# Values added by tiles on GpSimd, one product with the constant matrix, and the text rows gathered batch by batch

## What is computed

```python
h = concat([scharr_edges(gray(x)), (U * s @ Vt)[x_txt]], axis=1)   # (16, 384, 256)
# attention, 16 heads, window of 128 rows back, on layernorm(h)
attn = softmax(where(mask, scores, -10000.0)) + 1e-9
h = h + (attn @ v) @ Wo.T + bo
# the 288 highest rows of 384 by a router score pass gelu(x @ w_block)
h = h + mixture_of_depths(layernorm(h))
# state space: h_t = ifft(lambda * fft(h_{t-1})).real + B u_t ; y = C h_t + D u_t
h = h + ssm(layernorm(h))
# shared expert + top 2 of 8 experts, 256 -> 1024 -> 256
h = h + shared_ffn(x3) + sum_of_two_experts(x3)
```

## Time and profile before

| | us |
|---|---|
| median of 3 runs | 2071.47 |
| lowest, highest | 2069.86, 2071.95 |
| the profiled execution | 2072.98 |
| its span, first to last instruction | 2071.20 |
| 0 to 229.2: start, sequences 0 and 1 | 229.2 |
| 229.2 to 1213: twelve sequences in the loop | 983.8 |
| 1213 to 1436: the last sequences | 223.0 |
| 1436 to the end: experts | 635.2 |

### The profile page before, as it was taken

The page is one execution under the profiler, slowest core; times in us unless marked ns, Lnnn a source line. Parts: engine busy times, 40 slices in busy tenths (PEclk is TensorE's granted clock), DMA queues, the critical chain, the costliest instruction groups (busy, mean ns, idle before and its releaser), DMA issues.

```text
span 2071.2 us, 45656 instructions
## 1 busy us (share of the span) xinstructions
PE 1918.9 (93%) x14039; PEld 1626.8 (79%) x14120; DVE 1358.2 (66%) x3782; ACT 1066.4 (51%) x2510; POOL 782.1 (38%) x1269
## 2 busy tenths in 40 slices
PE   3679999999999999999999999888999999999997
PEld 3456777777777777777777777667999999999997
DVE  4657676777777777777777767654665565555653
ACT  0346455555555554555655655541664554655643
POOL 4012333343243233332432432324454454545544
PEclk8789999999999999999999999999999999999999
DMA  4320220211202212112122021111532232323222
GB/s 133 82 53 26 62 55 23 69 43 41 69 23 61 59 32 54 52 32 69 32 52 67 24 61 38 24 57 36 164 89 45 41 89 46 85 44 89 46 44 40
DMA packets 81092, 116.58 MB, mean 56 GB/s; under 512 B 20964, under 2 KB 61508, under 8 KB 78724
## 3 DMA queue, kind: packets, MB, share of 16 engines
q1 hardware_dynamic: 54372, 84.16, 15.1%
q0 software_dynamic: 23360, 27.91, 8.0%
q10 hardware_dynamic: 3312, 3.94, 0.6%
HBM read 51.58 MB, written 26.71 MB: 38 GB/s over the span
## 4 chain that ended last, share of the span: by engine, by line
PE 63%; issue 12%; DVE 11%; POOL 9%; ACT 2%; DMA 1%; POOLq 1%; ACTq 1%; DVEq 0%
PE ps L1956 14%; PE ps L1764 7%; PE ps L1968 5%; PE ps L1969 5%; PE ps L1967 5%; PE ps L1635 4%; POOL slot_rows L695 4%; PE ps L1607 3%; PE ps L1692 3%; PE ps L1712 2%; PE ps L1684 2%; PE ps L1754 2%; PE ps L1815 2%; PE ps L1777 2%; PE ps L1749 2%
## 5 line engine op out<-in xcount | busy, mean ns | idle before, releaser
L838 ACT ACTIVATE prob<-ps,mx 128x256 f32<-128x256 f32 (+1 forms) x768 | 294.3, 441 | 204.3 <-DVE mx L1194 198.6
L957 ACT ACTIVATE hid_hi<-ps,b 128x256 fp32r<-128x256 f32 x408 | 203.4, 499 | 286.3 <-PE ps L1956 286.3
L1194 DVE TENSOR_REDUCE mx<-ps 128x2 f32<-128x512 f32 (+1 forms) x384 | 227.6, 597 | 161.9 <-PE ps L1684 140.4
L1537 DVE TENSOR_TENSOR hid_lo<-hid_full,hid_hi 128x256 fp32r<-128x256 f32 x408 | 171.5, 425 | 145.7 <-ACT hid_full L960 142.0
L830 ACT ACTIVATE pT<-ps 128x512 f32<-128x512 f32 (+1 forms) x384 | 202.0, 531 | 120.3 <-PE ps L1692 79.4
L751 POOL DMA_INDIRECT result<-yb,idx_o x102 | 177.2, 1737 | 172.5 <-DVE yb L1554 150.7
L1967 PE MATMUL ps<-w_hi,hid_hi 128*128 128x256 f32 x816 | 233.5, 286 | 0.0
L1969 PE MATMUL ps<-w_hi,hid_lo 128*128 128x256 f32 x816 | 229.4, 281 | 0.0
L1968 PE MATMUL ps<-w_lo,hid_hi 128*128 128x256 f32 x816 | 229.3, 281 | 0.0
L1692 PE MATMUL ps<-ident,prob 128*128 128x128 f32 x1280 | 208.3, 277 | 6.2 <-ACT prob L838 6.0
L1684 PE MATMUL ps<-ks,qs 96*128 96x512 f32 (+1 forms) x384 | 201.3, 524 | 4.2 <-ACT prob L838 4.2
(11 more groups left out here) (310 smaller groups left out, 4244.0 us busy)
## 6 DMA issues: line engine op xcount, KB each, us to landing
w_raw<-in_w SPq DMA_DIRECT2D x16, 1024.0 KB
xin<-in_x SPq DMA_DIRECT2D x32, 384.0 KB
ks<-k_hi SPq DMA_DIRECT2D x256, 48.0 KB, 2.1
qs<-q_hi SPq DMA_DIRECT2D x120, 96.0 KB, 2.2
ks<-k_lo SPq DMA_DIRECT2D x128, 48.0 KB, 2.1
xn_rows<-xc SPq DMA_DIRECT2D x16, 384.0 KB, 2.5
result<-h SPq DMA_DIRECT2D x16, 384.0 KB
qs<-q_lo SPq DMA_DIRECT2D x60, 96.0 KB, 2.2
```

The costliest lines, as they stand in the source:

```text
L838: ins = act.activation(prob[:, s % PB, hh, w], ps[:, s % 2, hh * 2 * P + w.start:(hh + 1) * 2 * P], ACT.Exp, bias=mx[:, s % 2, hh:hh + 1])
L957: act.activation(hid_hi[:, f], ps[:, f % 4, 0:CHUNK], ACT.Gelu_apprx_tanh, bias=b1[half][:, f:f + 1])
L1194: dve.tensor_reduce(mx[:, s % 2], sc, AX_X, ALU.max, negate=True).then_inc(max_done.sem, 1)
```

## The change

The sum over the tiles of v is made by two additions on GpSimd (vsum), and TensorE makes one product in slot SUMV = 6 in place of three; VectorE copies it in slot 7. gather_text(b+2) is issued in GpSimd's sequence b, between dispatch and chain_deviations, through a copy of the batch's column of ids, into one buffer u_rows; batch 1 is gathered at the start. powers uses st for its helper rows, and the wait for the stacks in slot 1 of sequence 0 goes. split_router moves to slot 15 of sequence 0.

```diff
+SUMV = 6
-        u_all = sb("u_all", [P, NB, R])
+        id_col = sb("id_col", [P, 1], I32)
+        u_rows = sb("u_rows", [P, R])
+        vsum = room("vsum", [P, D])
...
         @block.gpsimd
-            def gather_text(b, done):
-                pool.indirect_dma_start(u_all[:, b, :], None, t["U"],
-                                        bass.IndirectOffsetOnAxis(ids[:, b:b + 1], axis=0)
-                                        ).then_inc(done.sem, 16)
+            def gather_text(b):
+                pool.wait_ge(ub_ready.sem, ub_ready.at(b - 1, 1))
+                pool.tensor_copy(id_col[:], ids[:, bass.ds(b, 1)]).then_inc(id_ready.sem, 1)
+                pool.wait_ge(id_ready.sem, id_ready.at(b - 1, 1))
+                pool.sem_inc(pool_go.sem, 1)
+                pool.indirect_dma_start(u_rows[:], None, t["U"], bass.IndirectOffsetOnAxis(id_col[:, 0:1], axis=0)
+                                        ).then_inc(u_gathered.sem, 16)
...
+            def add_values(b):
+
+                heads = vsum[:].rearrange("p (h d) -> p h d", h=NH)
+                pool.wait_ge(v_ready.sem, v_ready.at(b, 1))
+                pool.tensor_tensor(heads, vaug[:, 0, :, 0:DK], vaug[:, 1, :, 0:DK], ALU.add).then_inc(vsum_step.sem, 1)
+                pool.wait_ge(vsum_step.sem, vsum_step.at(b, 1))
+                pool.tensor_tensor(heads, heads, vaug[:, 2, :, 0:DK], ALU.add).then_inc(vsum_ready.sem, 1)
+
+            def sequence(b, att, late, chain, head, ahead):
+                if att:
+                    add_values(b)
                 if late and att:
                     dispatch(b - 2)
+                if ahead:
+                    gather_text(b + 2)
                 if chain:
                     if att:
                         chain_deviations(b - 1, 1)
...
-            for b in range(1, NB):
-                gather_text(b, u_gathered)
+            gather_text(1)
             residual(0)
...
-            sequence(0, True, False, False, True)
+            sequence(0, True, False, False, True, True)
...
+            with pool.Fori(2, NB - 2) as b:
+                sequence(b, True, True, True, True, True)
+            sequence(NB - 2, True, True, True, True, False)
...
         @block.scalar
             def text_rows(b):
                 act.wait_ge(uT_ready.sem, uT_ready.at(b, 0))
-                act.activation(ub[:, 0:R], u_all[:, bass.ds(b, 1), :], ACT.Copy).then_inc(ub_ready.sem, 1)
+                act.wait_ge(u_gathered.sem, u_gathered.at(b, 16))
+                act.activation(ub[:, 0:R], u_rows[:], ACT.Copy).then_inc(ub_ready.sem, 1)
...
-            act.wait_ge(u_gathered.sem, u_gathered.at(0, 16 * (NB - 1)))
             sequence(0, True, False, False, True, first=True)
...
         @block.vector
             def powers(n):
-                dve.tensor_scalar(rot[:, 0, 0:m], turn[:, 0, 0:m], re, None, ALU.mult)
-                dve.tensor_scalar(rot[:, 1, 0:m], turn[:, 0, 0:m], im, None, ALU.mult)
+                dve.tensor_scalar(st[:, 0, 0:m], turn[:, 0, 0:m], re, None, ALU.mult)
+                dve.tensor_scalar(st[:, 1, 0:m], turn[:, 0, 0:m], im, None, ALU.mult)
...
                     if first and s == 1:
                         eigenvalues()
-                        for pair in range(PAIRS):
-                            dve.wait_ge(stacked[pair].sem, stacked[pair].at(b, stacked[pair].per))
...
-                    if att and s == 2:
+                    if att and s == SUMV + 1:
                         values_sum(b)
...
                     if first and s == CONV:
+                        split_router()
                         split_shared()
...
-            dve.wait_ge(late_loaded.sem, late_loaded.at(0, NLATE))
-            split_router()
             sequence(1, True, False, True, True, True)
...
         @block.tensor
-            def values_sum(b, first, last):
-
-                pe.wait_ge(v_ready.sem, v_ready.at(b, 1))
+            def values_sum(b):
+
+                pe.wait_ge(vsum_ready.sem, vsum_ready.at(b, 1))
                 pe.wait_ge(h1_ready.sem, h1_ready.at(b, 0))
-                for i in range(first, last):
-                    ins = pe.matmul(ps[:, 5, D:2 * D].rearrange("p (h d) -> p h d", h=NH), ones9[:], vaug[:, i, :, 0:DK],
-                                    start=(i == 0), stop=(i == NT - 1))
-                if last == NT:
-                    ins.then_inc(sumv_done.sem, 1)
+                pe.matmul(ps[:, 5, D:2 * D], ones9[:], vsum[:], start=True, stop=True).then_inc(sumv_done.sem, 1)
...
-                    if att and s == BLOCK:
-                        values_sum(b, 1, NT)
                     if late and s == BLOCK:
                         down(b - 2, 0, chained, head)
...
-                    if att and s == TURN0:
-                        values_sum(b, 0, 1)
+                    if att and s == SUMV:
+                        values_sum(b)
```

More of the change, by code:

```diff
@@ L292, in build @@
         ids_loaded = dma_signal("ids_loaded", 0)
-        u_first = dma_signal("first_u_gathered", 0)
-        u_gathered = dma_signal("u_gathered", 0)
+        u_gathered = dma_signal("u_gathered", 16)
+        id_ready = signal("text_id_ready", 1)
         ub_zeroed = signal("ub_zeroed", 0)
@@ L318, in build @@
         v_ready = signal("v_ready", 1)
+        vsum_step = signal("tiles_of_values_added", 1)
+        vsum_ready = signal("vsum_ready", 1)
         sumv_done = signal("sumv_done", 1)
@@ L605, in _ @@
         def _(pool):
-            def gather_text(b, done):
-                pool.indirect_dma_start(u_all[:, b, :], None, t["U"],
-                                        bass.IndirectOffsetOnAxis(ids[:, b:b + 1], axis=0)
-                                        ).then_inc(done.sem, 16)
+            def gather_text(b):
[5 more added lines that the diff above has]
+                                        ).then_inc(u_gathered.sem, 16)
             pool.wait_ge(ids_loaded.sem, ids_loaded.at(0, 16))
-            gather_text(0, u_first)
+            pool.indirect_dma_start(u_rows[:], None, t["U"], bass.IndirectOffsetOnAxis(ids[:, 0:1], axis=0)
+                                    ).then_inc(u_gathered.sem, 16)
             pool.wait_ge(band_ready.sem, band_ready.at(0, 1))
@@ L718, in sequence @@
                     residual(b + 1)
-            for b in range(1, NB):
-                gather_text(b, u_gathered)
+            gather_text(1)
             residual(0)
             pool.wait_ge(slots_cleared.sem, slots_cleared.at(0, 48))
-            sequence(0, True, False, False, True)
+            sequence(0, True, False, False, True, True)
             pool.wait_ge(late_loaded.sem, late_loaded.at(0, NLATE))
[L726 to L731, removed]
+            sequence(1, True, False, True, True, True)
+            with pool.Fori(2, NB - 2) as b:
+                sequence(b, True, True, True, True, True)
+            sequence(NB - 2, True, True, True, True, False)
+            sequence(NB - 1, True, True, True, False, False)
+            sequence(NB, False, True, True, False, False)
+            sequence(NB + 1, False, True, False, False, False)
             def gather_rows(j, n):
@@ L1054, in powers @@
                 dve.scalar_tensor_tensor(out=turn[:, 0, n:n + m], in0=turn[:, 1, 0:m], scalar=nim,
-                                         in1=rot[:, 0, 0:m], op0=ALU.mult, op1=ALU.add)
+                                         in1=st[:, 0, 0:m], op0=ALU.mult, op1=ALU.add)
                 link(dve.scalar_tensor_tensor(out=turn[:, 1, n:n + m], in0=turn[:, 1, 0:m], scalar=re,
-                                                   in1=rot[:, 1, 0:m], op0=ALU.mult, op1=ALU.add), setup_step, 0)
+                                                   in1=st[:, 1, 0:m], op0=ALU.mult, op1=ALU.add), setup_step, 0)
                 dve.tensor_scalar(im, den, 2.0, None, ALU.mult)
@@ L1142, in split_shared @@
                 dve.wait_ge(sw1_rounded.sem, sw1_rounded.at(0, 1))
-                dve.tensor_tensor(sw1_lo[:], sw1, sw1_hi[:], ALU.subtract)
+                dve.tensor_tensor(sw1_lo[:], sw1, sw1_hi[:], ALU.subtract).then_inc(shared_split.sem, 1)
             def split_router():
+                dve.wait_ge(late_loaded.sem, late_loaded.at(0, NLATE))
                 link(dve.tensor_copy(rw_hi, rw[:]), setup_step, 0)
-                dve.tensor_tensor(rw_lo, rw[:], rw_hi, ALU.subtract).then_inc(shared_split.sem, 1)
+                dve.tensor_tensor(rw_lo, rw[:], rw_hi, ALU.subtract)
             def turned_rests(b):
```

2 lines of the change are left out of this document (removed).

## The result

The change makes the kernel slower: 2101.7 us (median of four, 2096.4 to 2109.5) against 2071.7 (four, 2069.9 to 2072.9). The ratio is 1.0146, interval 1.0117 to 1.0175: +30 us where the forecast was +14.6. The profiled execution took 2096.35 us, the lowest of its four; its span is 2094.6, that is +23.4 on the span before. The two traces add up as follows.

The account below looks back on a forecast made before the run. GpSimd's program order was taken to set the pace between slots 2 and 12, TensorE elsewhere. 25.2 + 10.2 - 8.2 - 12.5 = +14.7 us on 2072.98 gave 2087.7 profiled, 2086.2 as median; range 2068 to 2112 us.

Parts of the forecast that it names:

- the clock term: Loop, TensorE behind its idle before slot 12's transposes: granted clock falls in half of the passes, +10.2 us (0 to 20.4).
- the gather: Loop, GpSimd between dispatch and chain_deviations: gather_text adds 2.1 us in each of twelve passes, +25.2 us.
- Rival (c): Loop: the clock falls in every pass, 2096.4 us in all; chance 0.1.
- (a): Start: the stall at 37.5 to 50 us has nothing to do with GpSimd and stays, 2098.7 us; chance 0.25.
- rival (b): Loop: the clock never falls, 2076.0 us in all; chance 0.15.
- VectorE's wait: Start, slot 1: powers writes to st, so the wait for all stacks to land goes, -8.2 us.
- The products at the border and the additions: Loop: dropped ones9 products, the new product in slot 6 and the two GpSimd additions all lie off the path, 0.
- the idle before slot 12: Sign in the loop: TensorE's idle before the transposes of slot 12 is 2.5 us or more.
- the idle before down(0): Sign in the loop: TensorE still waits for gelu before down(0); an earlier start there would show the forecast wrong.
- the start: Before the loop: the waiting of VectorE on the stacks and ACT's stall both go, -20.7 us together.
- The stall: Start: ACT's xT held until 49.99 us; with fourteen gathers fewer on GpSimd the hold-up goes, -12.5 us (0 to -15).
- The coincidence at its end: Start: the hold-up of xT ends 0.8 us after GpSimd's last work, taken as evidence that GpSimd's gathers cause it.

Follow-up runs that it names:

- half: Changed kernel with the gather split: copy of ids and its wait ahead of the scatters, only the indirect DMA behind them; 2083.4 us, kernel before 2059.0.
- delay_3: Kernel before with three more small GpSimd steps ahead of the Newton steps of chain_deviations(b-1, 1); 2092.7 us, kernel before 2072.6.
- after: The changed kernel's profiled execution on the first chip; 2096.35 us, median of its four runs 2101.7.
- after_again: The changed kernel, unchanged, run and traced on a second chip; 2100.5 us, kernel before 2057.8, ratio 1.0200.
- warm: Changed kernel with nine unused identity products on TensorE ahead of the transposes of slot 12 in every loop pass; 2077.4 us, kernel before 2059.3.
- powers_only: Kernel before with only the change's lines for powers, the stacked wait and split_router; 2047.8 us, kernel before 2057.8.
- late_gathers: Kernel before with its gathers 2 to 15 placed behind residual(0) in place of ahead of it; 2060.9 us (one run), kernel before 2072.6.
- text_only: Kernel before with only the change's gathering of text rows by batch (u_rows, id_col, gather_text); 2099.5 us, kernel before 2059.3.
- pad_exact: Changed kernel with an unused buffer of 3808 bytes that puts the experts' buffers at their old addresses; 2110.2 us, kernel before 2059.0.
- sum_only: Kernel before with only the change's lines for vsum, SUMV and values_sum; 2059.1 us, kernel before 2059.3, ratio 1.0000.
- before_again: The kernel before, unchanged, run and traced on a second chip; 2056.9 us (one run), kernel before 2057.8.

## Why the prediction was wrong, and where it was right

**The step that failed is the clock term.** It said "I take a fall in half of the passes: 6 x 1.7 = +10.2 us; ends 0 and 12 x 1.7 = 20.4". The loop's +51.6 us less the gather's 25.2 leaves 26.4, above even the upper end. The mechanism was right, and the price of one fall nearly so: half has twelve at 1.7 us each, delay_3 six at 1.8, after 19 stretches at 1.3 and after_again 24 at 1.5. What was wrong was the number: one fall in about half of the passes is what an idle of 1.79 us brings (delay_3), and I put it on one of 2.6 us (measured 2.4), because the trace before had one gap of 1.99 with a fall and one of 1.90 without. But 2.6 is longer than the gap that had a fall, which speaks for a fall in every pass. Rival (c) had that, and is the best account of the loop, though its 20.4 us are still 6 short. Its total of 2096.4 us comes near only because the experts' 10 us, which it did not know of, went the other way; and (a), 2098.7, is nearest to the median by luck, with a stall that is gone in the trace. Two things more were in nobody's sum: falls that last 6.8 us (four in after, six in after_again), and those behind only 0.53 us of idle (as many again). One of the second kind was there to read in the trace before, at 301.27.

By the rule of the Trainium skill ("TensorE: Matmul & The Clock Gate", "Why this matters for your kernels", gaps above about 3 us) neither delay_3 nor half should have lost anything to the clock. The traces differ: falls behind 1.79 us in five of twelve passes, behind 1.98 in every pass. The measurement decides, and rival (b), to which that rule leads, falls.

**Right.** The gather: 2.10 us a pass, twelve times, measured as 2.10; warm's pass gives 2.2. VectorE's wait: -8.2 forecast, -8.0 at the second residual of powers_only and -10.0 in its time. The products at the border and the additions: 0 forecast, ratio 1.0000 (0.9991 to 1.0010). All of it where the prediction said it would show: the chain, the idle before slot 12 (2.4 us, where it named 2.5 or more), the idle before down(0). That the start agrees so well on the first chip, -20.9 against -20.7, is luck in part: about -10.7 of it is the stall and -10.2 the rest, where the terms were -12.5 and -8.2.

**Right, but not everywhere.** The stall: -12.5 forecast, about -10.7 in xT's start on the first chip, -11.7 us in late_gathers. On the three chips on which the kernel before takes 2057 to 2059 us there is no stall to lose, and text_only's start was even 2.5 us longer there (second residual at 136.2 against 133.7, one trace each). "The coincidence at its end" was the right sign: the stall hangs on the run of gathers. What holds TensorE is open. Not GpSimd's being busy as such, since late_gathers has gathers beside the same transposes; no semaphore in the code ties them; and why one kind of chip shows it, no view tells.

**Not in the prediction.** The experts' -10.3 us, from 3808 bytes less ahead of their buffers. Without it the change costs 2110.2 - 2059.0 = 51.2 us (pad_exact) in place of 42.6 (after_again). An edit that frees memory moves every later buffer; the prediction costed the instructions alone. Of the rest, the +1.1 us in sequence 1 go with the sum: that sequence takes 80.7 us in sum_only and 78.7 to 79.2 in powers_only, before_again and text_only. The +1.9 us in the pass behind the twelve are no fall in it: its first unit starts 2.4 us after the residual in place of 1.0, behind a fall late in the pass before (at 1235.5). half, which has none there, takes 81.7.

## What to carry to other kernels

Work put behind a wait for landings on an engine whose order sets the pace costs its whole length; ask where that engine waits longest and put it there (2.1 us a pass against nothing). A gap of the busiest engine has two prices, the time and the clock behind it, and the second grew from nothing at 0.94 us of idle to 2 to 3 us a pass at 2.4 and 3.0: fill the gap with idle products if it can't be closed. Before comparing two versions whose allocations differ, look whether the hot operands' addresses changed modulo 64, and give both the same; and compare two versions only on one chip.

## What the hardware did that I had not expected

- The granted clock fell to 0.50 behind 5 of 12 idles of 1.79 us and behind all twelve of 1.98 us, each time for 3.4 us; behind those of 2.4 and 3.0 us in 11 or all of 12, some for 6.8 us; and now and then behind only 0.53 us of idle (once in the twelve passes of before, six times in after_again).
- Products of 128x256 in fp32r followed each other every 113 ns where both operands lay at multiples of 64 bytes, every 118 ns where both lay 32 above one, 115 to 123 where one of them did. Products of the same shape in the up part took 120 ns in either layout.
- An indirect DMA behind a landing wait on GpSimd began 2.1 us after the scatters' end, a small arithmetic instruction in the same place 1.5 us.
- A run of fifteen indirect gathers on GpSimd goes with a hold-up of TensorE of 10 to 12 us on the first chip and on two of the five after it: before the projections if the gathers end at 47 us, before TensorE's first transposition if they end at 23, not at all if all but one begin at 34.6 or later.
